# A decoder layer on one core: projections four pairs ahead, scores three, and side products spread over other steps

## The reference

```
x  = x + attention(layernorm(x))          # 16 heads of 64, rmsnorm inside, softmax over 256 keys
x  = x + cross(layernorm(x), ctx)         # one head of 128, 512 context rows per batch, softmax over 512
x  = x + ffn(layernorm(x))                # 128 -> 512 -> 128, weights and activations rounded to 8-bit grids
q = h @ wq / 8; k = h @ wk; v = h @ wv    # per head, then softmax(q k^T) v, and w_out over all heads
```

## Time and profile before

| | |
|---|---|
| profiled execution, device time | 396.12 us |
| its span, first to last instruction | 394.2 us |
| granted TensorE clock, mean | 1.000 of 2.4 GHz |
| instructions | 9104 |
| projections, batch 1 to batch 7 | six batches, 56.5 to 318.3 us of the span |

### The profile page before, as it was taken

One profiled execution on the slowest core, in us unless ns is written; L12 is line 12 of the kernel. 1 busy time (PEld: TensorE's weight loads), 2 busy tenths in 40 slices (PEclk: granted clock), 3 DMA queues, 4 the chain that ended last, 5 costly groups with the idle time before them and its releaser, 6 DMA issues.

```text
span 394.2 us, 9104 instructions
## 1 busy us (share of the span) xinstructions
PE 379.1 (96%) x3012; PEld 286.3 (73%) x3012; DVE 323.8 (82%) x776; ACT 259.0 (66%) x805; POOL 164.1 (42%) x179
## 2 busy tenths in 40 slices
PE   8999999999999999999999999999999999998975
PEld 7778777777777777777777767777778777776422
DVE  4988779869897789869896889869895998766994
ACT  4976676666668566766677656767676768725674
POOL 3665444534544345525554345434454344511000
PEclk9999999999999999999999999999999999999999
DMA  7500000001000100001000100001000000000003
GB/s 233 153 17 2 2 2 0 3 2 40 2 3 2 40 0 0 0 0 40 0 0 0 40 0 0 0 0 40 0 0 0 27 2 2 2 2 0 0 2 106
DMA packets 12310, 7.50 MB, mean 19 GB/s; under 512 B 1280, under 2 KB 11264, under 8 KB 12288
## 3 DMA queue, kind: packets, MB, share of 16 engines
q1 hardware_dynamic: 11856, 6.69, 5.7%
q10 hardware_dynamic: 432, 0.52, 0.4%
HBM read 6.16 MB, written 1.05 MB: 18 GB/s over the span
## 4 chain that ended last, share of the span: by engine, by line
PE 66%; DVE 19%; issue 9%; ACT 2%; DVEq 1%; DMA 1%; POOL 1%; POOLq 0%; ACTq 0%
PE turned_bank L474 13%; PE o_bank L483 12%; PE score L464 12%; PE acc_bank L490 5%; DVE negmax L925 3%; DVE pT L932 3%; PE side_bank L447 3%; PE q_bank L447 3%; PE q_bank L448 3%; PE q_bank L449 3%; PE side_bank L541 3%; DVE h_max L1248 2%; PE side_bank L448 2%; PE side_bank L449 2%; PE side_bank L537 2%
## 5 line engine op out<-in xcount | busy, mean ns | idle before, releaser
L1292 POOL TENSOR_TENSOR prob<-prob,rinv 128x512 f32<-128x512 f32 x128 | 132.8, 1045 | 146.4 <-DVE rinv L929 146.4
L749 ACT ACTIVATE prob<-score,negmax 128x256 f32<-128x256 f32 x252 | 117.6, 475 | 71.7 <-DVE negmax L925 70.0
L925 DVE TENSOR_REDUCE negmax<-score 128x2 f32<-128x512 f32 x126 | 85.9, 682 | 26.8 <-PE score L464 25.4
L932 DVE COPY pT<-turned_bank 128x512 f32<-128x512 f32 x124 | 84.2, 679 | 7.0 <-PE turned_bank L474 6.6
L474 PE MATMUL turned_bank<-ident,prob 128*128 128x128 f32 x496 | 81.0, 286 | 1.7 <-DVE pT L932 1.2
L474 PEld LDWEIGHTS turned_bank<-ident,prob 128*128 128x128 f32 x496 | 52.0, 141 | 33.6 <-issue 24.2
L483 PE MATMUL o_bank<-pT,v_sb 128*64 128x256 f32 x512 | 69.4, 392 | 0.6 <-ACT oT L740 0.6
L749 ACT ACTIVATION_READ_ACCUMULATOR prob<-score,negmax 128x1 f32 x252 | 51.2, 203 | 0.0
L483 PEld LDWEIGHTS o_bank<-pT,v_sb 128*64 128x64 f32 x512 | 31.1, 136 | 19.9 <-issue 8.2
L740 ACT ACTIVATE q_hi<-q_bank 128x512 fp32r<-128x512 f32 x63 | 38.2, 606 | 10.6 <-PE q_bank L449 9.7
L917 DVE TENSOR_TENSOR q_lo<-q_bank,q_hi 128x512 fp32r<-128x512 f32 x63 | 42.8, 680 | 0.0
(11 more groups left out here) (230 smaller groups left out, 618.7 us busy)
## 6 DMA issues: line engine op xcount, KB each, us to landing
c_sb<-in_ctx_dram SPq DMA_DIRECT2D x8, 256.0 KB, 3.0
x_sb<-in_x_dram SPq DMA_DIRECT2D x8, 128.0 KB, 2.8
out_dram<-xn_all SPq DMA_DIRECT2D x4, 256.0 KB, 2.9
big<-in_L_attn_wk_dram ACTq DMA_DIRECT2D x2, 256.0 KB, 4.7
big<-in_L_attn_wq_dram SPq DMA_DIRECT2D x2, 256.0 KB, 5.7
big<-in_L_attn_wv_dram SPq DMA_DIRECT2D x2, 256.0 KB, 6.3
wo_sb<-in_L_attn_w_out_dram SPq DMA_DIRECT2D x1, 512.0 KB, 7.7
w_sb<-in_L_ffn_w_dram SPq DMA_DIRECT2D x2, 256.0 KB, 4.7
```

What stands on the lines that cost most here:

```text
L749: last = nc.scalar.activation(prob[:, slot, t, :], banks[r][:, t * S:(t + 1) * S], ACT.Exp, bias=negmax[:, slot, t:t + 1], scale=1.0, accu ...
L925: nc.vector.tensor_reduce(negmax[:, slot], banks[r][:].rearrange("p (t k) -> p t k", k=S), X_AXIS, ALU.max, negate=True).then_inc(max_done, 1)
L932: nc.vector.tensor_copy(pT[:, slot].rearrange("p k q -> p (k q)"), bank[:]).then_inc(pT_done, 1)
L1292: nc.gpsimd.tensor_tensor(prob[:, slot], prob[:, slot], rinv[:, slot].unsqueeze(2).to_broadcast([P, QT, S]), ALU.mult).then_inc(prob_done, 1)
```

## The change

In the new step PE starts with the first head of pair j turned, and then does the projections of pair j+4, the side product of place 0, `project_out` of pair j-2, the second head of pair j turned, the values of pair j-1, the side product of place 1 and last the scores of pair j+3. The streams of ACT, DVE and POOL are put in an order that goes with it. The projections of pair 3 and the scores of pair 2 move ahead of the first step. The side products get other places; each of the steps of a mid batch now has one in place 0.

```diff
-PLACE = {(0, 0): "W2", (0, 1): "TC", (1, 0): "W1", (2, 0): "W3", (2, 1): "TX", (3, 0): "QX", (3, 1): "TH",
-         (4, 0): "SX0", (4, 1): "PX0", (5, 0): "SX1", (5, 1): "PX1", (6, 0): "UX", (6, 1): "OX", (7, 0): "V0"}
+PLACE = {(0, 0): "TC", (0, 1): "W2", (1, 0): "W1", (1, 1): "W3", (2, 0): "TH", (2, 1): "TX", (3, 0): "QX",
+         (3, 1): "SX0", (4, 0): "PX0", (4, 1): "SX1", (5, 0): "PX1", (5, 1): "UX", (6, 0): "OX", (7, 0): "V0"}
@@ PE, step
-                if more_q:
-                    project_qk((j + 3) % PAIRS, ..., q_banks[(j + 3) % 2])
-                if task := side_at(kind, j, 0):
-                    side(kind, b, 1 - parity, i, task)
-                if cross and j == 1:
-                    project_out(PAIRS - 1)
-                if more_scores:
-                    pe.wait_ge(q_lo_done, g + 3)
-                    pe.wait_ge(exp_done, 2 if kind == "first" and j == 0 else 2 * g + 4)
-                    scores(j % 2)
                 pe.wait_ge(prob_done, 2 * g + 1)
                 wait(pe, pT_done, copied_before(kind, g, j, 0))
                 turn_probs(2 * j % 8, turned_in(kind, j, 0))
+                if ahead(kind, j, 4):
+                    if kind == "first" and j == 0:
+                        pe.wait_ge(wqk_lo_done, 4)
+                    project_qk((j + 4) % PAIRS, ..., q_banks[j % 2])
+                if task := side_at(kind, j, 0):
+                    side(kind, b, 1 - parity, i, task)
                 if not (kind == "first" and j < 1):
                     wait(pe, o_done, g - 1)
-                if j != 1 and not (kind == "first" and j < 2):
+                if not (kind == "first" and j < 2):
...
                     project_out((j - 2) % PAIRS)
-                if task := side_at(kind, j, 1):
-                    side(kind, b, 1 - parity, i, task)
+                pe.wait_ge(prob_done, 2 * g + 2)
+                pe.wait_ge(pT_done, copied_before(kind, g, j, 1))
+                turn_probs(2 * j % 8 + 1, turned_in(kind, j, 1))
...
                     values((j - 1) % PAIRS, (slot, slot + 1), 1 - parity if j == 0 else parity)
-                if not no_scores:
-                    turn_probs(2 * j % 8 + 1, turned_in(kind, j, 1))
+                if task := side_at(kind, j, 1):
+                    side(kind, b, 1 - parity, i, task)
+                if ahead(kind, j, 3):
+                    pe.wait_ge(q_lo_done, g + 4)
+                    pe.wait_ge(exp_done, 2 * g + 6)
+                    scores((j + 1) % 2)
@@ PE, ahead of the steps
             scores(1, (o_bank, acc_bank))
+            project_qk(3, 0, q_banks[1])
+            pe.wait_ge(q_lo_done, 3)
+            pe.wait_ge(exp_done, 2)
+            scores(0)
@@ ACT, step: exps(0), side place 0, exps(1), split_hi, side place 1, copy of oT
-                if ahead(kind, j, 3):
-                    split_hi((j + 3) % 2, q_banks[(j + 3) % 2])
...
+                if ahead(kind, j, 4):
+                    act.wait_ge(q_raw, g + 5)
+                    split_hi(j % 2, q_banks[j % 2])
@@ DVE, step: maxima(0), keep_turned(first), maxima(1), statistics or normalise, side place 0,
@@   invert_sums(first), keep_turned(second), invert_sums(second), residual, split_lo, side place 1
+                if prepare and j == 1:
+                    normalise(0, tiles(xn1), tiles(x_sb[:, 1 - parity]), b + 2, xn1_done)
...
+                if ahead(kind, j, 4):
+                    dve.wait_ge(q_hi_done, g + 5)
+                    split_lo(j % 2, q_banks[j % 2])
@@ POOL, step
-                if prepare and j == 0:
+                if prepare and j == 1:
                     inverse_root(0, b + 2)
-                if cross and j == 1:
+                if cross and j == 2:
                     inverse_root(1, b)
```

More of the change, by code:

```diff
@@ L801, in step @@
                     exps(1, (2 * j + 5) % 8)
+                if ahead(kind, j, 4):
+                    act.wait_ge(q_raw, g + 5)
+                    split_hi(j % 2, q_banks[j % 2])
+                if task := side_at(kind, j, 1):
+                    side(kind, b, 1 - parity, task)
                 if not (kind == "first" and j < 1):
@@ L855, in _ @@
             exps(1, 1)
+            act.wait_ge(q_raw, 4)
+            act.wait_ge(score_raw, 4)
+            split_hi(1, q_banks[1])
             act.wait_ge(max_done, 3)
@@ L1055, in step @@
                 more_scores = ahead(kind, j, 2)
[L1056 to L1063, removed]
-                if cross and j == 2:
[L1065 to L1069, removed]
-                if cross and j == 1:
-                    residual(b, 1 - parity)
+                if cross and j == 2:
+                    aggregate(1, b, *PLAIN_NORM)
                 if more_scores:
@@ L1075, in step @@
                     maxima(0, (2 * j + 4) % 8)
+                if kind == "mid" and j == PAIRS - 1:
+                    aggregate(2, b, *PLAIN_NORM)
                 dve.wait_ge(pT_raw, 2 * g + 1)
@@ L1081, in step @@
                     invert_sums(3)
[L1082 to L1085, removed]
                 if more_scores:
@@ L1088, in step @@
                     maxima(1, (2 * j + 5) % 8)
-                if kind == "first" and j == 0:
-                    dve.wait_ge(load_x[1], 16)
-                    statistics(0, tiles(x_sb[:, 1]), 2)
                 if prepare and j == 0:
[L1093 to L1099, removed]
+                    if kind == "first":
+                        dve.wait_ge(load_x[1], 16)
+                    else:
+                        dve.wait_ge(load_x[1 - parity], (i + 2) * 16)
+                    statistics(0, tiles(x_sb[:, 1 - parity]), b + 2)
+                if cross and j == 2:
+                    normalise(1, tiles(xn2), tiles(x1_sb), b, xn2_done)
+                if task := side_at(kind, j, 0):
                     side(kind, b, 1 - parity, task)
-                if kind == "mid" and j == PAIRS - 2:
-                    dve.wait_ge(side_free, side_index(kind, b, "OX") + 1)
+                if kind == "mid" and j == PAIRS - 1:
+                    cross_norm(b)
                 if more_scores:
@@ L1105, in step @@
                     invert_sums((2 * j + 4) % 8)
-                if not no_scores:
-                    dve.wait_ge(pT_raw, 2 * g + 2)
-                    keep_turned(2 * j % 4 + 1, turned_in(kind, j, 1))
+                if prepare and j == 0:
+                    aggregate(0, b + 2, *FIRST_NORM)
+                if prepare and j == 1:
+                    normalise(0, tiles(xn1), tiles(x_sb[:, 1 - parity]), b + 2, xn1_done)
+                dve.wait_ge(pT_raw, 2 * g + 2)
+                keep_turned(2 * j % 4 + 1, turned_in(kind, j, 1))
+                if more_scores:
+                    dve.wait_ge(exp_done, 2 * g + 6)
+                    invert_sums((2 * j + 5) % 8)
+                if cross and j == 1:
+                    residual(b, 1 - parity)
+                if kind == "mid" and j == PAIRS - 2:
+                    dve.wait_ge(side_free, side_index(kind, b, "OX") + 1)
+                if ahead(kind, j, 4):
+                    dve.wait_ge(q_hi_done, g + 5)
+                    split_lo(j % 2, q_banks[j % 2])
                 if kind == "mid" and j == PAIRS - 2:
                     statistics(2, x2_of(b), b)
-                if kind == "mid" and j == PAIRS - 1:
-                    cross_norm(b)
+                if task := side_at(kind, j, 1):
+                    side(kind, b, 1 - parity, task)
                 if kind == "last" and j == 0:
@@ L1153, in _ @@
             invert_sums(2)
+            dve.wait_ge(q_hi_done, 4)
+            split_lo(1, q_banks[1])
             over_batches(dve, step)
```

22 lines of the change are left out of this document (5 added, 17 removed).

## The result

The changed kernel takes 390.76 us (median of 4, 390.68 to 391.19) where the kernel before took 396.66 beside it (396.37 to 397.19): a ratio of 0.9848, with an interval of 0.9836 to 0.9861, or 5.9 us less. Forecast were 2.6 us less, in a range that holds the time. So the direction was right, and the gain is more than twice the one that was worked out.

The account below looks back on a forecast made before the run. TensorE was taken as the bound, running nearly without a gap. Waits -3.8, neighbours 0, first steps +1.1, last batch -0.8 and +0.9 sum to -2.6 us, from median 396.38 to 393.8 us; range 390.0 to 397.6.

Parts of the forecast that it names:

- the size of the waits: TensorE in six mid batches: waits of 4.1 us in all, of which the change was to win 3.8.
- Neighbours: Cost of changed neighbours among TensorE's groups in a mid batch: taken as 0, with ends -0.6 and +0.6 us.
- New waits in the middle: Small waits the new order might bring over the six mid batches: 0.3 us allowed.
- the one with moved waits: Rival, chance 0.14: waits only move, W2 and TX miss their operands, 0.4 a batch; 396.2 us, no change.
- the one with VectorE as the bound: Rival, chance 0.13: scores wait for VectorE's late maxima, 0.3 in steps 2, 6 and 7, six times; 399.2 us.
- First steps: Start of the kernel: second turned head at 18.8 us, not 17.9, and later scores of pair 3; +1.1 us.
- Last batch: Last batch: -0.8 us from waits that go, +0.9 past the last scores, with project_out of step 7 waiting for oT.
- The likeliest case: The forecast case, whole kernel: 393.8 us, chance 0.58, own range 391.8 to 395.8.
- The third rival, cheaper neighbours: Chance 0.15: values to scores cost 0.97 and fp32r side products nothing extra, -0.5 a batch over all 8; 390 us.

Follow-up runs that it names:

- e5: The kernel before with VectorE's normalise(0) of the next batch moved from the start of step 3 to the start of step 1: 400.24 us, ratio 1.0089.
- e3: The new kernel with project_out between values and scores in the 15 steps with place 0 filled and place 1 free: 394.01 us, ratio 0.9928.
- e4: The kernel before with side products TC and W2 exchanged in step 0, TC now at place 0: 398.12 us, ratio 1.0033.
- e6: The kernel before with VectorE taking cT_lo ahead of the aggregate and split_lo in step 0: 395.31 us, ratio 0.9961.
- e7: The kernel before with the edits of e5 and e6 together: 403.20 us, ratio 1.0168.
- e1: The kernel before, in its old order, with all new places of the side products and normalise(0) at step 1: 407.98 us, ratio 1.0277.
- e8: The new kernel with VectorE taking the low part of pair 3 behind the second maxima of the first step: 390.36 us, ratio 0.9842.
- e9: The new kernel; in the last batch ACT copies oT ahead of place 1's side product, and project_out of steps 4 and 5 precedes PX0 and PX1: 389.21 us.

## Why the prediction was half the gain

**The step that failed is the size of the waits: "the six hold 0.27 + 3 x 0.65 + 2 x 0.92 = 4.1 us of waits".** It rested on "these pitches come again in every batch to within 0.01 us unless something is late, so what is longer is a wait". A wait that comes in every batch is in the usual pitch. Per batch the waits were:

| wait | counted | found, us | shown by |
|---|---|---|---|
| W1, with its slower first pass | yes | 0.38 or 0.66 |, gone in the new timeline |
| values of step 1 | yes | 0.155 | 1.01 in the new timeline |
| SX0 | half | 0.22 | e5 |
| TH | no | 0.10 | e5 |
| QX | no | 0.16 | traces alone |
| TX | no | 0.05 | traces alone |

The five that every batch has are 0.685. The turned head that waits in step 1 is itself 0.03 shorter than usual (0.38, not 0.41), which leaves 0.655, six times 3.9. W1 adds 0.38 three times and 0.66 twice. That is 6.4 us against the 4.1 of the forecast, and what was not counted (TH, QX, TX and half of SX0) makes the difference. For QX and TX no kernel of its own was run. QX, first before and then after, stands behind projections that start at 154.35 and at 155.39; so it starts 0.86 and 0.80 behind them, and it takes 0.23 and 0.11 to its second pass:
```profile
155.21 0.39 PE L447 MATMUL side_bank<-x2T_hi,c_hi 128*128 128x256 f32 x1
155.44 0.28 PE L448 MATMUL side_bank<-x2T_lo,c_hi 128*128 128x256 f32 x1
```
```profile
156.19 0.28 PE L447 MATMUL side_bank<-x2T_hi,c_hi 128*128 128x256 f32 x1
156.30 0.28 PE L448 MATMUL side_bank<-x2T_lo,c_hi 128*128 128x256 f32 x1
```
project_out and TX take 0.47 and 0.34 in a mid batch before; with TH's two matmuls of the same shape in that place, batch 0 has 0.45 and 0.31. The wait table names none of TH, QX, TX and SX0.

**Neighbours: 0 a batch, measured -0.1, by two errors that cancel.** The step with no side product, forecast at 4.21 and 0.3 a batch in all, is 4.12 against 4.26 before: -1.15 over 8 steps. Values to scores, taken as 1.06, is 1.01, the cheap bound but for 0.04. Turned head to values, taken as 0.59 from the earlier trace rows, is 0.53: that row's turned head stood right behind scores and paid for it. Against that stands what a side product adds to its step. Behind the fp32 values the first pass of an fp32r one costs 0.10 more, as forecast at 0.09 (148.47 to 148.81 against 145.77 to 146.01), but the values and the scores are then no neighbours either, and W3 adds 0.90 to its step where one such product added 0.69 before. It is 0.2 for each of W2, W3, SX0 and SX1, 0.2 for UX too (1.92 now, 1.72 before) and 0.15 for TX, in all +1.15 where the forecast had +0.36. So both terms were over three times as large, and that they cancel is luck. The -0.1 that is left over can't be assigned by this count.

Six times -0.1 and the 6.4 of waits are 7.0; by the windows of the earlier trace rows the six batches fell by 261.73 - 254.79 = 6.94. From batch 0 to batch 1 the same count holds: six steps there have place 1 free and gain 0.14 to 0.15 each, two with a side product there give 0.1 back, and 0.13 of wait at the values of step 1 goes, 0.9 of the 0.96. The prediction had counted nothing there but this wait.

The prediction weighed a rule of the Trainium skill, "TensorEngine Tiling (Array Packing)", section Key Properties: a change of mode drains TensorE. The trace and e3 agree: one change fewer at the same work is worth 0.20 us, not the 0.09 at which the entry alone had put it.

**New waits in the middle: 0.3 allowed, none found.** W2, at most 0.1 ahead of its operand by the forecast, had 0.4: cT_lo ends at 184.79, W2 starts at 185.23. e4, e6 and e7 moved TC or cT_lo forward in the old order, and waits stayed or came. A reading that fits them, though no run tests it alone: the new step 7 has the cross norm ahead of the inverted sums and not last, and the scores close the step, so the maxima that open VectorE's step find their queue short. The two rivals of more waits, the one with moved waits and the one with VectorE as the bound, both need late maxima; they were 0.10 late. e1 and e7 are what these rivals look like, in the old order.

**First steps: +1.1 forecast, +1.30 measured,** by the forecast's own chain: the second turned head at 19.72, which less the late start of 0.85 is 18.87 (18.8 forecast), then the exponentials. e8 confirms the cause named, the low part of pair 3 ahead of the first maxima, by getting 0.54 back.

**Last batch: -0.8 + 0.9 forecast; measured +1.10 from its mark on, and -0.39 at the values of step 1, ahead of the mark; 0.7 in place of 0.1.** The wait for oT in step 7 came as named (0.52 by its row, from 341.63 to 342.76 against 0.44 a full 0.68). What the forecast took at 0 and 0.15 are PX0 and PX1: each starts 0.75 behind its turned head (330.21 to 330.96), against 0.44 for an unhindered neighbour. In the last batch no projections stand between, so that the exponentials of SX0, which the mid batches hide behind 0.80 us of projections, are in the open. ACT in the last batch:
```profile
330.13 0.69 ACT L754 ACTIVATE x_prob<-side_bank,x_negmax 128x512 f32<-128x512 f32 x1 [1.38 <-DVE x_negmax L1007]
```
It ends at 330.82, and PX0 starts at 330.96. Scores waited 0.2 once, and project_out ran twice 0.1 slower. e9 takes back 1.37 by exactly these places.

**The chances.** The likeliest case happened in its signs but for one: the six batches take 254.8 us, not 257.9, and the time lies outside the case's own range by 1.0 us (390.76 against 391.8 to 395.8). The third rival, cheaper neighbours, names 390 and thus nearly the right total, for a reason that didn't happen: neighbours gave 0.1 a batch and not 0.5, and fp32r side products did pay behind the values.

## What to carry to other kernels

A pitch that repeats in every round is not thereby free of waits. Take the same instruction where nothing can be late (the first or last round, or a kernel in which its operand comes early) and use that as the usual pitch; otherwise many waits of 0.1 to 0.2 us are counted as work. And places for side work can't be judged without the order of the queues that serve them: the same table of places gained in one order and lost 11 us in the other.

## What the runs showed of the hardware

At a change of the array's shape TensorE does not load weights ahead. In the new kernel the second turned head's first load starts at 46.83, ahead of its matmul at 46.94; that of the values starts with its matmul at 47.47, and that of the scores at 48.48, after idle time of 0.38:
```profile
46.83 0.47 PEld L474 LDWEIGHTS turned_bank<-ident,prob 128*128 128x128 f32 x4
47.47 0.63 PEld L483 LDWEIGHTS o_bank<-pT,v_sb 128*64 128x64 f32 x8 [0.17 <-issue]
48.48 0.19 PEld L464 LDWEIGHTS score<-q_hi 64*128 64x128 f32 x2 [0.38 <-issue]
```
In the steps of the new kernel the first load is 0.00 to 0.03 ahead of its matmul wherever the shape changes and 0.10 to 0.23 ahead elsewhere, with one exception: projections behind a turned head, where fp32 changes to fp32r, have 0.03. The change from the values' shape to the scores' costs no more than one of the two to the full array: 1.01 both times. A wait for a semaphore leaves the same mark as a change of shape, a first fp32r pass that is 0.1 longer, and that mark helps to tell the hidden waits at QX and SX0 from work. It tells only where the neighbour is the same in both cases, since the projections behind a turned head have it too (0.20 against 0.12 in the earlier trace rows) with neither a wait nor a change of shape.

`normalise` of 128x128 fp32 in SBUF, on VectorE, takes 0.34 us or up to 1.08, and the longer ones all lie beside GpSimd's work. In e5 the two at 192.50 took 1.62, and each of them ends 0.08 behind one of GpSimd's two scalings (193.05 and 194.04):
```profile
192.01 2.04 POOL L1292 TENSOR_TENSOR prob<-prob,rinv 128x512 f32<-128x512 f32 x2 [0.60 <-DVE rinv L929]
```
In the new kernel the two of step 2 find GpSimd idle (193.80 to 195.93) and take 0.34 each; of the two in step 1, the first starts at 189.04, ahead of a scaling at 189.20, and takes 0.32, and the second, inside that scaling, takes 1.06.
```profile
194.79 0.60 DVE L954 TENSOR_SCALAR xn<-x_sb,mv,rstd 128x128 f32<-128x128 f32 x2
```
In the executions of the kernel before, of the new one and of e5, each with 32 of them, all that GpSimd's work doesn't touch took 0.34 to 0.35, and none that took longer was free of it. The Trainium skill, "GPSIMD Engine Reference", section Specifications, has GpSimd share its SBUF interfaces with VectorE, with contention for VectorE's instructions of two kinds. The rows agree that the two contend; which of the kinds `normalise` is, no run here shows.
